# A perceiver block with a top-2 expert layer on one core: the stretch between the last exponentials of the cross attention and the first expert product, rewritten on all five engines

## The reference

```python
x = x + cross_attention(layernorm(x), ctx)   # 257 keys per sequence, biases, key mask
x = x + causal_self_attention(layernorm(x))  # 32 keys, rotary embedding on q and k
x = x + experts(layernorm(x))                # 8 experts of hidden width 1368

# experts: every 128 tokens are a group; softmax over 8 logits, the two largest are chosen;
# in a group an expert takes 32 tokens: first choices in order, second choices behind them
p1 = cumsum(m1) - m1;              m1 = m1 * (p1 < 32)
p2 = cumsum(m2) - m2 + sum(m1);    m2 = m2 * (p2 < 32)
combine  = gate1 * onehot(idx1) x onehot(p1) + gate2 * onehot(idx2) x onehot(p2)
dispatch = combine != 0
inputs   = dispatch^T @ x
out      = combine @ ((gelu(inputs @ w0) * (inputs @ w1)) @ wo)
```

## Time and profile before

| | us |
|---|---|
| three runs | 554.91, 552.29, 553.98; median 553.98 |
| span of the profiled execution | 553.1 |
| end of batch 31's exponentials, from the span's start | 276.7 |
| start of the first expert product | 349.4 |
| last instruction | 553.1 |

### The profile page before, as it was taken

The page is one execution under the profiler, slowest core; times in us unless marked ns, Lnnn a source line. Parts: engine busy times, 40 slices in busy tenths (PEclk is TensorE's granted clock), DMA queues, the critical chain, the costliest instruction groups (busy, mean ns, idle before and its releaser), DMA issues.

```text
span 553.1 us, 18277 instructions
## 1 busy us (share of the span) xinstructions
PE 497.3 (90%) x6637; PEld 455.6 (82%) x6637; DVE 400.3 (72%) x1003; ACT 324.7 (59%) x839; POOL 253.9 (46%) x341
## 2 busy tenths in 40 slices
PE   1897999999999999999956657899999999999996
PEld 1776888888888888988845546899999999999995
DVE  2544456666767766676766797699999999999973
ACT  1455767667757775775722206756676666666650
POOL 4133344444364344536310120566767667766650
PEclk9989999999999999999996655799999999999998
DMA  6523111111111111110018000255645666457202
GB/s 181 170 78 80 42 34 29 43 40 33 33 39 39 20 39 38 39 20 3 3 9 299 1 0 1 80 163 180 191 145 170 221 191 185 127 187 227 81 1 76
DMA packets 58125, 48.91 MB, mean 88 GB/s; under 512 B 20942, under 2 KB 49744, under 8 KB 58064
## 3 DMA queue, kind: packets, MB, share of 16 engines
q1 hardware_dynamic: 58064, 48.09, 29.8%
HBM read 46.86 MB, written 1.08 MB: 87 GB/s over the span
## 4 chain that ended last, share of the span: by engine, by line
PE 79%; ACT 6%; DVE 5%; issue 5%; DMA 3%; SPq 1%; DVEq 0%; ACTq 0%; POOL 0%; POOLq 0%
PE bank L223 20%; PE bank L225 18%; PE bank L224 18%; PE bank L606 5%; PE bank L584 4%; PE bank L630 3%; PE bank L541 2%; ACT Pr L1059 2%; DMA last_prob<-Pr 2%; PE bank L989 2%; DMA w_raw<-in_L_xattn_Wk 1%; PE bank L761 1%; ACT PTd L1152 1%; PE bank L723 1%; PE bank L734 1%
## 5 line engine op out<-in xcount | busy, mean ns | idle before, releaser
L223 PE MATMUL bank<-XT_lo,W_hi 128*128 128x256 f32 (+1 forms) x352 | 100.2, 285 | 1.3 <-ACT CT L1253 1.3
L224 PE MATMUL bank<-XT_hi,W_lo 128*128 128x256 f32 (+1 forms) x352 | 99.8, 284 | 0.0
L225 PE MATMUL bank<-XT_hi,W_hi 128*128 128x256 f32 (+1 forms) x352 | 99.6, 283 | 0.0
L2000 POOL TENSOR_TENSOR W_lo<-raw,W_hi 128x256 fp32r<-128x256 f32 (+1 forms) x88 | 88.4, 1005 | 7.1
L1919 POOL TENSOR_TENSOR Pr<-Pr,rinv 128x1028 f32<-128x1028 f32 x31 | 59.0, 1903 | 47.0 <-DVE rinv L1404 46.3
L1059 ACT ACTIVATE Pr<-Sc,nmax 128x257 f32<-128x257 f32 x128 | 63.8, 502 | 23.8 <-DVE nmax L1393 19.5
L1393 DVE CUSTOM_DVE_ANT_0 Sc<-bank,mask_add 128x257 f32<-128x257 f32 x128 | 47.0, 423 | 40.8 <-PE bank L584 17.8
L1850 DVE TENSOR_TENSOR hid_lo<-hid,hid_hi 128x256 fp32r<-128x256 f32 (+1 forms) x88 | 72.5, 824 | 1.5 <-ACT hid_hi L1302 1.5
L1998 POOL CAST W_hi<-raw 128x256 fp32r<-128x256 f32 (+1 forms) x88 | 39.4, 448 | 73.4 <-PE bank L225 37.0
L1820 DVE TENSOR_TENSOR W_lo<-raw,W_hi 128x512 fp32r<-128x512 f32 (+1 forms) x88 | 69.1, 788 | 4.9 <-ACT W_hi L1226 1.3
L223 PEld LDWEIGHTS bank<-XT_lo,W_hi 128*128 128x128 f32 (+1 forms) x352 | 66.3, 188 | 1.6 <-issue 1.6
(11 more groups left out here) (237 smaller groups left out, 1345.7 us busy)
## 6 DMA issues: line engine op xcount, KB each, us to landing
raw<-in_L_ffn_w_kernel SPq DMA_DIRECT2D x32, 512.0 KB, 4.7
ctx_raw<-in_ctx SPq DMA_DIRECT2D x32, 256.0 KB, 2.8
raw<-in_L_ffn_wo_kernel SPq DMA_DIRECT2D x16, 512.0 KB, 5.8
raw<-in_L_ffn_w_kernel SPq DMA_DIRECT2D x16, 344.0 KB
last_prob<-Pr SPq DMA_DIRECT2D x128, 1.0 KB, 1.8
raw<-in_L_ffn_wo_kernel SPq DMA_DIRECT2D x8, 256.0 KB
x_sb<-in_x SPq DMA_DIRECT2D x4, 256.0 KB, 5.9
VL_all<-vl_rows SPq DMA_DIRECT2D x8, 128.0 KB
```

Of the source, the lines that this page charges most:

```text
L223: pe.matmul(dst, a_hi, b_lo, start=first, stop=False)
L224: pe.matmul(dst, a_lo, b_hi, start=False, stop=False)
L225: return pe.matmul(dst, a_hi, b_hi, start=False, stop=last)
L2000: po.tensor_tensor(W2_lo[0:w, m % RW, :], raw2[0:w, t, :], f(W2_hi[0:w, m % RW, :]), ALU.subtract)\
```

## The change

In words:

- **Last key.** For batches 28 to 31 SP moves the raw exponential of the last key and the raw sum as soon as the exponentials are there (`p_ready`), and no longer waits for the normalisation; VectorE inverts the moved sums (`invert_last`) and multiplies (`scale_last`) before GpSimd forms `Ot`.
- **Last normalisation.** VectorE divides two of the four groups of batch 31 (256 columns each), GpSimd the other two.
- **VectorE's order.** `choose`, `slots_of`, `weigh`, the layer norm, the early tiles' steps and others are cut into single instructions (`norm_step(t, who, n)`, `choose(t, n)`, and so on), and the list alternates between tiles, so that a step seldom follows the one that it needs. A counter (`mark`, `need`) takes the place of the wait behind each step.
- **PE's and ACT's lists** are put in another order, the end of the pipeline's last step with them; most PSUM banks of the tail change, so that values of `z` have a bank of their own (`values_at`).
- **Last dispatch mask.** For `z` the mask is made directly from slots and places by two 128x256 comparisons (`disperse_last`), ahead of the combine weights.
- **Combine weights** of tiles 6 and 7 are turned behind the first two `up` of the expert stage; the first slices of the expert weights are split earlier on ACT and VectorE.

The diff, cut to what the text below speaks of:

```diff
-PICK, PLACE = 8, 5
+LATE = B - BT
...
-        return front(t) if isinstance(t, int) and t >= TT - 2 else bk[7]
+        return bk[7] if not isinstance(t, int) or t < TT - 3 else bk[5] if t == TT - 3 else front(t)
...
+    def values_at(t):
+
+        return bk[7] if isinstance(t, int) and t == TT - 1 else front(t)
 
...
-            sp.wait_ge(sm["p_normed"], b + 1)
+            if isinstance(b, int) and b >= LATE:
+                sp.wait_ge(sm["p_ready"], 4 * b + 4)
+            else:
+                sp.wait_ge(sm["p_normed"], b + 1)
...
+            elif isinstance(b, int) and b == B - 1:
+                pe.wait_ge(sm["p_normed"], B)
+                pe.wait_ge(sm["last_normed"], 1)
+                pe.wait_ge(sm["s_read"], 4 * B)
+                pe.wait_ge(sm["b_pT_act"], TT - 2)
+                pe.wait_ge(sm["b_pT_dve"], TT - 2)
+                pe.wait_ge(sm["pt1_ready"], b)
...
-            pe.wait_ge(sm["b_v"], t + 1)
+            if values_at(t) is front(t):
+                pe.wait_ge(sm["b_v"], t + 1)
...
-        y_, z = TT - 2, TT - 1
-        project_self(y_, True)
-        after_self(y_ - 1, False)
+        v_, y_, z = TT - 3, TT - 2, TT - 1
+        turn_probs(B - 2, (B - 2) % 4, 0)
+        turn_probs(B - 2, (B - 2) % 4, 1)
+        project_self(y_, False)
+        self_outputs(v_)
         turn_probs(B - 1, (B - 1) % 4, 0)
         turn_probs(B - 1, (B - 1) % 4, 1)
-        turn_qk(y_)
         outputs(B - 2, (B - 2) % 4, -1)
+        project_out(v_)
         outputs(B - 1, (B - 1) % 4, -1)
         turn_last(z)
+        project_self(y_, True)
+        turn_qk(y_)
+        project_cross(z)
+        turn_router(v_)
         scores(y_)
-        project_cross(z)
-        project_out(y_ - 1)
+        logits(v_)
+        positions(0, EARLY)
         turn_norm(z)
         project_self(z, False)
+        project_self(z, True)
         turn_self_probs(y_)
-        project_self(z, True)
         turn_qk(z)
         self_outputs(y_)
         scores(z)
-        turn_router(y_ - 1)
-        logits(y_ - 1)
+        project_out(y_)
+        dispatch(0)
+        dispatch(1)
         turn_self_probs(z)
-        project_out(y_)
+        turn_router(y_)
+        positions(v_, y_)
+        logits(y_)
         self_outputs(z)
-        positions(0, EARLY)
+        turn_weights_of(0)
+        dispatch(2)
         project_out(z)
-        turn_router(y_)
+        dispatch(3)
         turn_router(z)
-        logits(y_)
-        dispatch(0)
-        positions(y_ - 1, y_)
-        dispatch(1)
+        positions(y_, z)
         logits(z)
-        dispatch(2)
-        positions(y_, z)
-        dispatch(3)
         dispatch(4)
-        turn_weights_of(0)
         turn_weights_of(1)
+        dispatch(v_)
+        positions(z, TT)
+        dispatch(y_)
         turn_weights_of(2)
-        positions(z, TT)
-        dispatch(y_ - 1)
-        dispatch(y_)
         dispatch(z)
-        turn_weights_of(3)
...
+                if half_ == 0 and q == 1:
+                    pe.wait_ge(sm["ct_read"], TT // 2)
...
         up(*place(1))
+        turn_weights_of(TT // 2 - 1)
...
+        split(0, 1)
         self_exp(z)
-        split_self(y_)
-        keep_router(y_ - 1)
+        keep_inputs(0)
+        keep_router(y_)
         spread_probs(z)
+        keep_inputs(1)
         split_self(z)
-        keep_router(y_)
-        router_exp(y_ - 1)
         router_exp(y_)
+        keep_weights_of(0)
+        keep_inputs(2)
+        split(0, 2)
         keep_router(z)
-        keep_inputs(0)
+        keep_inputs(3)
         router_exp(z)
-        keep_inputs(1)
-        keep_inputs(2)
-        keep_inputs(3)
-        keep_weights_of(0)
+        keep_inputs(4)
         keep_weights_of(1)
-        keep_inputs(4)
-        keep_weights_of(2)
-        keep_inputs(y_ - 1)
-        for n in range(3):
-            split(0, n)
+        keep_inputs(v_)
         keep_inputs(y_)
         keep_inputs(z)
-        keep_weights_of(3)
+        keep_weights_of(2)
...
+            if m == 0:
+                keep_weights_of(TT // 2 - 1)
...
+            elif n == 6:
+                need(("place0", t), ("place1", t))
+                mark("past", ve.tensor_scalar(past[:, :], both(place_, t), float(CAP), 4096.0, ALU.is_ge, ALU.mult))
+            else:
+                need(("slot", t), "past")
+                mark("reach", ve.tensor_tensor(past[:, :], both(slot_of, t), past[:, :], ALU.add))
...
+        def disperse_last():
+
+            need("reach")
+            ve.wait_ge(sm["r_x_made"], TT - 2)
+            mark("disp0", ve.tensor_scalar(disp[:, (TT - 1) % 2, :], slot_no, past[:, 0:1], None, ALU.is_equal))
+            need("disp0")
+            ve.scalar_tensor_tensor(out=disp[:, (TT - 1) % 2, :], in0=slot_no, scalar=past[:, 1:2],
+                                    in1=f(disp[:, (TT - 1) % 2, :]), op0=ALU.is_equal, op1=ALU.add).then_inc(sm["r_disp"], 1)
...
         def normalise_last():
 
             ve.wait_ge(sm["p_inv"], B)
-            r = (B - 1) % 2
-            ve.tensor_tensor(Pr[:, r, :, 0:SC], Pr[:, r, :, 0:SC], rinv[:, r, :].unsqueeze(2).broadcast_to([P, G, SC]),
-                             ALU.mult).then_inc(sm["p_normed"], 1)
+            r, own = (B - 1) % 2, slice(0, G // 2)
+            ve.tensor_tensor(Pr[:, r, own, 0:2 * P], Pr[:, r, own, 0:2 * P],
+                             rinv[:, r, own].unsqueeze(2).broadcast_to([P, G // 2, 2 * P]), ALU.mult).then_inc(sm["last_normed"], 1)
+
+        def invert_last():
+            for moved in stats_moved:
+                ve.wait_ge(moved, 8 * HG * B)
+            ve.sem_inc(sm["turns_ve"], 1)
+            mark("last_inv", ve.reciprocal(last_inv[:, :], last_prob[:, TT - 1, :, 1]))
+
+        def scale_last():
+            need("last_inv")
+            ve.tensor_tensor(last_prob[:, TT - 1, :, 0], last_prob[:, TT - 1, :, 0], last_inv[:, :], ALU.mult)\
+              .then_inc(sm["last_scaled"], 1)
...
+        invert_sums(B - 1, (B - 1) % 4)
+        normalise_last()
+        keep_probs(B - 2, (B - 2) % 4)
+        share_early(0)
+        share_early(1)
+        turn_angles(y_, 0)
+        turn_angles(y_, 1)
+        turn_angles(y_, 2)
+        split_self(v_)
+        invert_last()
+        keep_probs(B - 1, (B - 1) % 4)
+        scale_last()
...
+        scale_scores(y_)
+        norm_step(z, "b", 4)
+        choose_early(1, 3)
+        max_scores(y_)
+        choose_early(1, 4)
...
+        scale_scores(z)
+        choose(v_, 5)
+        max_scores(z)
+        disperse(0)
+        less_max(z)
+        split_self(y_)
+        weigh(1, 0)
+        norm_step(y_, "c", 0)
+        choose(v_, 6)
+        norm_step(y_, "c", 1)
+        weigh(1, 1)
+        norm_step(y_, "c", 2)
+        choose(v_, 7)
+        norm_step(y_, "c", 3)
+        sum_probs(z)
+        weigh(1, 2)
+        invert_self(z)
+        choose(v_, 8)
+        scale_probs(z)
+        norm_step(y_, "c", 4)
+        disperse(1)
+        spread_probs(z)
+        choose(v_, 9)
+        weigh(2, 0)
+        weigh(2, 1)
+        weigh(2, 2)
+        disperse(2)
+        weigh(3, 0)
+        read_logits(y_)
+        split_self(z)
+        choose(y_, 0)
+        slots_of(v_, 0)
+        choose(y_, 1)
+        slots_of(v_, 1)
+        choose(y_, 2)
+        slots_of(v_, 2)
+        norm_step(z, "c", 0)
...
+        norm_step(z, "c", 4)
+        disperse(3)
...
+        read_logits(z)
+        slots_of(y_, 0)
+        choose(z, 0)
+        slots_of(y_, 1)
+        choose(z, 1)
+        slots_of(y_, 2)
+        choose(z, 2)
...
+        choose(z, 7)
+        weigh(y_, 0)
+        weigh(y_, 1)
+        weigh(y_, 2)
+        disperse(y_)
+        slots_of(z, 0)
+        slots_of(z, 1)
+        slots_of(z, 2)
+        choose(z, 8)
+        slots_of(z, 3)
+        choose(z, 9)
+        slots_of(z, 6)
+        slots_of(z, 4)
+        slots_of(z, 7)
+        disperse_last()
+        split(0, 1)
+        split(0, 2)
+        slots_of(z, 5)
+        weigh(z, 0)
+        weigh(z, 1)
+        weigh(z, 2)
...
+            if isinstance(t, int) and t == TT - 1:
+                po.wait_ge(sm["last_scaled"], 1)
+            else:
+                for moved in stats_moved:
+                    po.wait_ge(moved, 8 * HG * (BT * t + BT))
...
-            po.tensor_tensor(Pr[:, r % 2, :, 0:SC], Pr[:, r % 2, :, 0:SC], rinv[:, r % 2, :].unsqueeze(2).broadcast_to([P, G, SC]),
-                             ALU.mult).then_inc(sm["p_normed"], 1)
+            own = slice(G // 2, G) if isinstance(b, int) and b == B - 1 else slice(0, G)
+            n = 2 * P if isinstance(b, int) and b >= LATE else SC
+            po.tensor_tensor(Pr[:, r % 2, own, 0:n], Pr[:, r % 2, own, 0:n],
+                             rinv[:, r % 2, own].unsqueeze(2).broadcast_to([P, own.stop - own.start, n]), ALU.mult)\
+              .then_inc(sm["p_normed"], 1)
```

(40 more changed lines are left out.)

531 lines of the change are left out of this document (312 added, 219 removed).

## The result

The changed kernel takes 538.56 us (median of four runs, 535.71 to 542.80) beside 553.23 for the kernel before: a ratio of 0.9742, 95% interval 0.9702 to 0.9782, or 12 to 16.5 us. Measured again with six runs it is 538.93 beside 554.01, 0.9729 (0.9693 to 0.9766). Forecast was 541.1, with 535.5 to 546.5 as the range, so it came out as forecast, 2.5 us to the fast side. The profiled execution is the slowest of the four (542.80, span 541.0), and of the kernel before too (554.91, span 553.1): between the spans lie 12.1.

The account below looks back on a forecast made before the run. The expert stage was taken as PE-bound, the tail as a chain of handovers for z; legs of -5.6 - 1.3 + 1.9 + 5.1 - 1.8 - 11.2 = -12.9, with +0.9 and -0.9, gave 541.1 us from 553.98, range 535.5 to 546.5.

Parts of the forecast that it names:

- Leg 1: End of batch 31's exponentials to end of `Ot`: 12.70 to 7.1 us, the exponentials releasing the last key's transfer; -5.6.
- The halves: Last normalisation split between VectorE and GpSimd: possibly one after the other, but off the path; charged nothing, bound 1.0 us.
- Leg 2: End of `Ot` to end of y1: 7.76 to 6.5 us, less waiting on VectorE and faster products; -1.3.
- Leg 3: End of y1 to end of `scores(z)`: 11.05 to 12.9 us, z queued behind early tiles' positions and `self_outputs(y_)`; +1.9.
- Leg 4: End of `scores(z)` to end of `self_outputs(z)`: 9.27 to 14.4 us, z behind tile 6's steps and `dispatch(1)`; +5.1.
- Leg 5: End of `self_outputs(z)` to end of y2: 8.41 to 6.6 us, less waiting against weights and `dispatch(2)` ahead; -1.8.
- Leg 6: End of y2 to first expert product: 23.46 to 12.3 us, earlier `yTf`, positions and mask, interleaved steps; -11.2.
- That interleaving buys little: Rival, VectorE in the tail: interleaved steps still cost 0.24 each and VectorE becomes the bound; 545 to 549 us, chance 0.10.
- The full clock: Rival, PE in legs 3 to 6: denser work keeps the clock at 1.00, saving 5.2 us; 536, chance 0.08.
- the five queues: Rival: z behind other tiles' steps at five places costs 5.1 us each, against 9.5 summed; 557 us, chance 0.04.
- That nothing changes: Rival, expert stage: the gain comes back if that stage waits for its weights; no change, chance 0.03.
- Behind the tail: Expert stage's start: four transposes among the first expert's products at half clock cost +0.9 us.

Follow-up runs that it names:

- late_move: Changed kernel, but SP moves the last key's raw sums of batches 28 to 31 only after their batch's normalisation; ratio 0.9742 to the kernel before.
- sum_first: Changed kernel with leg 4 reordered: z's sum, division, transposes and outputs ahead of other tiles' steps on VectorE and PE; ratio 0.9665 to the kernel before.
- norm_first: Changed kernel with PE's turn_norm(z) ahead of positions(0, EARLY), and z's low part of y1 earlier on VectorE; ratio 0.9736 to the kernel before.
- weights_ahead: Changed kernel with the combine weights of tiles 4 and 5 turned ahead of z's positions, as before; ratio 0.9732 to the kernel before.
- whole_norm: Changed kernel with the last normalisation on VectorE alone, four groups of 256 columns; ratio 0.9718 to the kernel before.
- second profile: The changed kernel as it is, timed with six more runs and profiled again; 538.93 us, ratio 0.9729 to the kernel before.
- sum_again: Leg 4's reordering alone on the changed kernel, measured a second time; 536.81 us, ratio 0.9661 to the kernel before.
- both_again: Changed kernel with leg 3's and leg 4's reorderings together, measured a second time; 536.23 us, ratio 0.9638 to the kernel before.
- blocks: Changed kernel with leg 6's interleaving undone: VectorE does six steps of slots_of(y_), then eight of choose(z); ratio 0.9745 to the kernel before.
- after: The changed kernel's first measurement and profile, nothing altered; 538.56 us, ratio 0.9742 to the kernel before.
- both reorderings: Changed kernel with z's steps put ahead of other tiles' in leg 3 and leg 4; ratios 0.9716 and 0.9638 to the kernel before.

## Why the prediction was right, step by step

The mechanism was right, and three of six legs came within 0.4 us in the first profile. By its own steps:

- **Leg 1.** The release by the exponentials is there, and the landing comes 4.0 behind them, where I expected 5.2. The chain of the changed kernel:

```profile
279.47 1.80 DMA last_prob<-Pr
...
281.60 0.24 DVE last_inv L1896
281.84 0.54 DVE PT L1449
282.39 0.43 DVE last_prob L1900
```

  From the last issue to the landing are 1.80, not the 3.21 of the earlier trace rows, the 1.4 that I had kept as its bound. But the 1.4 is no gain of the change. Each move counts up its semaphore in sixteen parts, and in the trace of the kernel before fifteen parts of the last move are there 1.80 behind its issue and the sixteenth 3.21. It comes 1.3 to 1.7 behind the other fifteen in six of the fourteen profiles taken here, whatever the release: before, `late_move`, `sum_first`, `norm_first`, `weights_ahead` and `whole_norm`. There the four moves take 5.0 to 5.5 in all, in the other eight 3.9 to 4.4. VectorE stands idle for it, in `weights_ahead`, `whole_norm` and `sum_first`:

```profile
282.65 0.25 DVE L1896 RECIPROCAL last_inv<-last_prob 128x16 f32<-128x16 f32 x1 [0.87 <-issue]
```

```profile
281.47 0.25 DVE L1896 RECIPROCAL last_inv<-last_prob 128x16 f32<-128x16 f32 x1 [0.68 <-issue]
```

```profile
281.85 0.25 DVE L1896 RECIPROCAL last_inv<-last_prob 128x16 f32<-128x16 f32 x1 [0.92 <-issue]
```

  With the late part leg 1 is 6.9 to 7.2, which is the forecast's 7.1, and without it 6.3. So the release is worth what I summed, and the 0.8 beyond it in both profiles of the changed kernel is the luck of the execution. The Trainium skill ("SBUF — State Buffer", section "The DMA setup-cost knee") has a roughly fixed 2 us for a transfer. The traces agree for the eight profiles without the late part (1.8 to 2.1 for the last move) and not for the six with it (3.1 to 3.5).
- **The halves.** GpSimd's half took 1.55, where a full one of 128x1024 takes 1.90, while VectorE's half (0.69) had begun 0.04 before it. As I had it, nothing of it reached the path (`whole_norm`). The rule of the Trainium skill on the shared ports ("SBUF — State Buffer", section "Who interferes with whom") fits this, though no run here tells its waiting from its working.
- **Leg 2**, 0.45 short in my sum. y1 is no longer late behind tile 6's subtraction, but `x_sb` of `z` is behind tile 6's queries. VectorE's timeline: the addition starts at 287.95 though PE's products end at 287.2:

```profile
287.25 0.68 DVE L1547 TENSOR_TENSOR qTb<-bank,tab 128x512 f32<-128x512 f32 x1
...
287.95 0.41 DVE L1475 TENSOR_TENSOR x_sb<-bank,x_sb 128x256 f32<-128x256 f32 x1
```

- **Leg 3.** The transposes start 1.73 behind y1; I had 2.0. `norm_first` takes that away and 1.0 to 1.7 with it. The clock, which I let rise within the eighteen products (-0.9), stayed at 0.50 through them in both profiles (six products in 1.28 us, as at 0.50 in the earlier trace rows) and rose only behind them. So that term did not come, but neither did the +0.85 that I had charged for `self_outputs(y_)` at half clock: in the first profile it ran at 1.00 and took 1.08 (PE's timeline).

```profile
296.04 0.41 PE L225 MATMUL bank<-WT_lo,yT_hi 128*128 128x256 f32 x1
296.68 0.41 PE L225 MATMUL bank<-WT_lo,yT_hi 128*128 128x256 f32 x1
297.32 0.41 PE L225 MATMUL bank<-WT_lo,yT_hi 128*128 128x256 f32 x1
...
300.60 1.08 PE L795 MATMUL bank<-PTd,Vm 128*32 128x128 f32 x32 [0.43 <-ACT PTd L1187]
```

  Without that charge my 12.9 would be 12.05, and 11.8 with the transposes as they came; measured are 12.51. Some 0.7 is then missing elsewhere, perhaps in the -0.95 for a bank of its own, which no run tested. The 0.3 between the two profiles lies ahead of the products: in the second the clock fell only during the early tiles' positions, and the transposes start 1.43 behind y1.
- **Leg 4.** PE's and VectorE's timelines: the sum starts 5.94 behind the scores (forecast 5.9), and PE, standing at `dispatch(1)` for its mask, lets the ready `pr` wait 1.6 (forecast 1.7):

```profile
307.46 0.42 DVE L1475 TENSOR_TENSOR x_sb<-bank,x_sb 128x256 f32<-128x256 f32 x1 [1.48 <-PE bank L227]
...
309.01 0.69 DVE L1585 TENSOR_REDUCE sum<-pr 128x16 f32<-128x512 f32 x1
...
310.22 0.69 DVE L1911 TENSOR_TENSOR pr<-pr,inv 128x512 f32<-128x512 f32 x1
...
311.54 0.77 PE L913 MATMUL bank<-disp,y_hi 128*128 128x256 f32 x2 [3.26 <-issue]
...
312.54 1.06 PE L766 MATMUL bank<-tab,pr 128*128 128x128 f32 x4
```

  `sum_first` shows that this is the order's price, 4.6 beside these two profiles.
- **Leg 5**, 0.5 too dear in my sum. `project_out(z)` starts 0.8 behind the low part of the outputs that it needs, where I had charged 1.3 for the weights and the dispatch ahead of it. VectorE's and PE's timelines:

```profile
317.98 0.42 DVE L1509 TENSOR_TENSOR O2T_lo<-bank,O2T_hi 128x256 fp32r<-128x256 f32 x1 [0.68 <-ACT O2T_hi L1117]
...
319.19 0.41 PE L225 MATMUL bank<-WT_lo,O2T_hi 128*128 128x256 f32 x1
```

  In the second profile (5.62) these products run at full clock, 0.12 apart.
- **Leg 6**, the largest. ACT's, VectorE's and PE's timelines, to be read against the earlier trace rows:

```profile
325.50 0.38 ACT L1117 ACTIVATE yTf<-bank 128x256 f32<-128x256 f32 x1 [4.46 <-PE bank L816]
...
327.78 0.16 DVE L1707 CUSTOM_DVE_ANT_0 lg<-bank,zero 128x8 f32<-128x8 f32 x1
...
329.45 0.23 DVE L1741 TENSOR_SCALAR chosen<-tab,lowest 128x8 f32<-128x8 f32 x1
...
329.74 0.61 PE L899 MATMUL bank<-chosen,tab 128*128 128x16 f32 x2
...
332.63 0.48 DVE L1882 SCALAR_TENSOR_TENSOR disp<-tab,past,disp 128x256 fp32r<-128x256 f32 x1
```

  y2 to `yTf`: 1.9 in place of 5.9. Logits read to second mask: 1.9 in place of 3.5. Mask to positions: 0.06 in place of 4.7. These three are 10.3 of the 11.2. The pieces that I undid are worth less than my terms: interleaving 0.7 to 1.0 (1.6), the direct mask 0.5 to 0.75 (0.9), and one group of four transposes 0.8 to 1.1. The 4 us on `yTf` were not undone by themselves; they are read from the two traces.
- **The rivals.** That interleaving buys little holds at one place by half, but VectorE did not become the bound. The full clock did not come (0.50 to 0.67 in most of the tail), nor did the five queues cost 5 each: 1.7 and 4.6 at the most for the three in legs 3 and 4, and 0.8 for the one in leg 5; the one in leg 6 was not undone. That nothing changes is excluded by the interval.
- **Behind the tail** I had +0.9; the first profile has 1.4, the second 1.1. The granted clock stays at 0.50 for 5.3 and 4.8 us behind the first expert product there, and for 4.0 before, 3.9 to 6.1 over all profiles. At half the speed that is 0.6 and 0.4 of the loss, an estimate, and leaves 0.8 and 0.7 for the four transposes. Another stretch of half clock, 3.4 us long, lies 12 us before the end of the span in nine of the fourteen profiles, those of before and of the changed kernel among them, and is missing in the other five (`sum_first`, `sum_again`, `both_again`, `blocks`, `whole_norm`). Windows in the last products, first `after`, then `blocks`, where the clock is 1.00:

```profile
529.00:531.00 2.00, 1.99 (x5) 1.63 (x6) 0.00 (x0) 0.00 (x0) 0.00 (x0) 0.50 0.00 0
```

```profile
531.10:533.10 2.00, 2.00 (x10) 1.77 (x11) 0.56 (x2) 0.00 (x0) 0.00 (x0) 1.00 0.00 0
```

  At half the speed it costs some 1.7 us, an estimate. The two profiles of both reorderings, one kernel, differ by 2.7 us behind the first expert product (205.8 and 203.1), so that a difference of this size there tells nothing of a kernel.
